# A vision tower in split fp32: weight low parts moved from VectorE to GpSimd, the opening cut in halves

## The reference

```python
h = L0_tok(x)                                    # patches @ W_lin + b, class token, positions
h = h + L0_attn(layernorm(h))                    # 16 heads of 64, causal
h = h + L0_ffn(layernorm(h))                     # 256 -> 1024 -> 256
h = h + L1_attn(layernorm(h))                    # 16 heads of 64, not causal
h = h + L1_ffn(layernorm(h))                     # 8 experts 256 -> 1024 -> 256, times masked logits
...
    h = jnp.einsum('bsd,df->bsf', x, w1) + b1    # L0_ffn
    h = float2fix(h, 8)                          # round to 1/256
    h = pwlin_gelu_basic(h, 8, 8)                # 33 knots of gelu, linear between, rounded
    out = jnp.einsum('bsf,fd->bsd', h, w2) + b2
    return float2fix(out, 8)
```

## Time and profile before

| | |
|---|---|
| median of 3 runs | 944.38 us (944.03 to 945.27) |
| the profiled execution | 946.15 us |
| its span, first to last instruction | 944.4 us |
| PE busy | 919.1 us, 97% |
| DVE busy | 586.4 us, 62% |
| ACT busy | 557.6 us, 59% |
| POOL busy | 155.6 us, 16% |
| mean DMA rate | 36 GB/s |

### The profile page before, as it was taken

The page is one execution under the profiler, slowest core; times in us unless marked ns, Lnnn a source line. Parts: engine busy times, 40 slices in busy tenths (PEclk is TensorE's granted clock), DMA queues, the critical chain, the costliest instruction groups (busy, mean ns, idle before and its releaser), DMA issues.

```text
span 944.4 us, 19121 instructions
## 1 busy us (share of the span) xinstructions
PE 919.1 (97%) x7073; PEld 856.1 (91%) x7073; DVE 586.4 (62%) x1860; ACT 557.6 (59%) x1571; POOL 155.6 (16%) x173
## 2 busy tenths in 40 slices
PE   8999999999999999999999999999999999999998
PEld 8978988788877878888879999999999999999998
DVE  4677676749999776757667787554354534554333
ACT  4666474647664755656555655565556646575442
POOL 0332122211000221222210000711011111111012
PEclk9999999999999999999999999999999999999999
DMA  9310000001100210000001012102020111100001
GB/s 334 135 46 1 2 1 2 2 1 46 45 1 3 87 45 1 2 1 2 2 28 64 1 45 90 46 2 90 1 91 1 46 45 46 46 1 1 2 14 39
DMA packets 8800, 34.43 MB, mean 36 GB/s; under 512 B 642, under 2 KB 5122, under 8 KB 5380
## 3 DMA queue, kind: packets, MB, share of 16 engines
q1 hardware_dynamic: 8708, 33.22, 9.8%
HBM read 32.00 MB, written 1.21 MB: 35 GB/s over the span
## 4 chain that ended last, share of the span: by engine, by line
PE 44%; issue 34%; DVE 13%; POOL 6%; ACT 2%; POOLq 0%; DVEq 0%; ACTq 0%
PE D L609 15%; PE O L609 10%; POOL h L372 4%; PE O L804 4%; PE S L779 3%; PE T L790 3%; PE S L609 3%; PE D L631 2%; DVE probsT L1364 2%; DVE probs L1349 2%; PE O L725 2%; PE O L878 1%; POOL h L384 1%; DVE xc L1240 1%; DVE rt L1231 1%
## 5 line engine op out<-in xcount | busy, mean ns | idle before, releaser
L1620 DVE TENSOR_TENSOR hid<-work,hid 128x296 fp32r<-128x296 f32 x256 | 134.3, 551 | 178.5 <-ACT hid L1157 177.7
L609 PE MATMUL O<-hid,wslot 128*128 128x296 f32 (+2 forms) x1680 | 238.4, 300 | 0.0
L609 PEld LDWEIGHTS O<-hid,wslot 128*128 128x128 f32 x1680 | 231.2, 188 | 0.6
L609 PE MATMUL D<-xn,wslot 128*128 128x296 f32 (+2 forms) x1368 | 219.9, 307 | 0.0
L609 PEld LDWEIGHTS D<-xn,wslot 128*128 128x128 f32 x1368 | 197.7, 190 | 3.2 <-issue 0.3
L1153 ACT ACTIVATE work<-D,prm 128x296 f32<-128x296 f32 x128 | 66.1, 516 | 166.2 <-PE D L609 165.8
L1048 ACT ACTIVATE probs<-probs,negmax 111x111 f32<-111x111 f32 (+1 forms) x352 | 130.3, 372 | 29.9 <-DVE negmax L1349 29.4
L588 POOL TENSOR_TENSOR probs<-probs,rsum 111x444 f32<-111x444 f32 (+1 forms) x88 | 81.3, 925 | 360.9 <-DVE rsum L1357 360.9
L609 PE MATMUL S<-xn,wslot 128*128 128x296 f32 (+2 forms) x864 | 133.6, 301 | 0.0
L609 PEld LDWEIGHTS S<-xn,wslot 128*128 128x128 f32 x864 | 123.0, 189 | 0.1
L1349 DVE CUSTOM_DVE_ANT_0 probs<-S,maska 111x111 f32<-111x111 f32 (+1 forms) x352 | 73.1, 263 | 66.3 <-PE S L779 66.3
(11 more groups left out here) (180 smaller groups left out, 1174.5 us busy)
## 6 DMA issues: line engine op xcount, KB each, us to landing
raw<-in_moe SPq DMA_DIRECT2D x16, 1024.0 KB, 4.8
raw<-in_attn SPq DMA_DIRECT2D x7, 1024.0 KB, 4.9
work<-in_x SPq DMA_DIRECT2D x2, 1008.0 KB, 8.2
out<-h SPq DMA_DIRECT2D x4, 296.0 KB, 2.6
w2f<-in_attn SPq DMA_DIRECT2D x1, 1024.0 KB, 13.5
raw<-in_ffn SPq DMA_DIRECT2D x1, 1024.0 KB, 5.0
w2f<-in_ffn SPq DMA_DIRECT2D x1, 1024.0 KB, 5.0
raw<-in_x SPq DMA_DIRECT2D x2, 504.0 KB, 5.1
```

Of the source, the lines that this page charges most:

```text
L609: mm = pe.matmul(psum, a, b, start=(first and k == 0), stop=(k == 3 * n - 1))
L1620: nc.vector.tensor_tensor(moe_hid(s, 1), moe_g(s)[:, 0:w], moe_hid(s, 0).bitcast(F32), ALU.subtract).then_inc(m_hid, 1)
```

## The change

**On POOL**, between the scaling of the first attention and that of the second, three whole pieces are subtracted: `FIRST_W` + 6, + 7 and + 8, each as soon as ACT's high part of it is there. DVE's twelve quarters for them go. PE and SP wait for the same pieces as before, on POOL's semaphore.

**In the opening** the second chunk's patches are loaded, copied and subtracted in halves (`x1_half`, new semaphores `x1_in`, `x1_high`, `x1_low`), PE embeds the second chunk half by half for both banks, 18 warm-up matmuls stand in the place of 28, `variance(0, 0)` stands one embedding later, and on DVE and ACT the last chunk's and the query weight's parts stand ahead of the first layer norm's end.

**The bias row** is prepared in two pieces: four copies at unit 3, the subtraction at unit 4.

```diff
...
         x0_in = sem("x0_in")
+        x1_in = sem("x1_in")
+        x1_high = sem("x1_high")
+        x1_low = sem("x1_low")
         v0_in = sem("v0_in")
...
         LATE_W = FIRST_W + 4
+        POOL_LATE = [FIRST_W + 6, FIRST_W + 7, FIRST_W + 8]
         NPIECE = FIRST_W + len(weights)
...
 
+            if i in POOL_LATE:
+                return (pool_split, LATE_W - NSTART + POOL_LATE.index(i) + 1)
             if i >= LATE_W:
-                return (dve_split, i - LATE_W + 1 - past(i))
+                return (dve_split, i - LATE_W + 1 - past(i) - sum(k < i for k in POOL_LATE))
             return (start_split, i + 1) if i < NSTART else (pool_split, i - NSTART + 1)
...
 
+        def x1_half(t, k):
+
+            n = KF * CHUNKS[1][1] // 2
+            return t[:, k * n:(k + 1) * n]
+
         def piece_size(i):
...
                     dst, src = w_half(dst, 1), w_half(src, 1)
-                if i == 1:
+                if i == 2:
+                    n = KF // 2
+                    sp.dma_start(x1_half(dst, 0).rearrange("p (k n) -> p k n", k=n),
+                                 src[:, 0:n, :]).then_inc(x1_in, 16)
+                    dst, src = x1_half(dst, 1).rearrange("p (k n) -> p k n", k=n), src[:, n:KF, :]
+                elif i == 1:
                     n = KF // 2
...
             normalise(0)
-
+            for i in POOL_LATE:
+                if place_free(i):
+                    pool.wait_ge(*place_free(i))
+                split(i)
             normalise(1)
...
             pe.wait_ge(consts, 1)
-            for _ in range(28):
+            for _ in range(18):
                 pe.matmul(BO[0][:, 0:P], mean_w[:, :], mean_w[:, :], start=True, stop=True)
...
                 embed_part(0, dc, range(KF // 2, KF), False, True)
-            embed(1, 0)
+            pe.wait_ge(x1_low, 1)
+            for dc in range(KD):
+                pe.wait_ge(h_set, dc + 1)
+                embed_part(1, dc, range(KF // 2), True, False)
             mean(0, 0)
-            embed(1, 1)
+            pe.wait_ge(*piece_split(2))
+            for dc in range(KD):
+                embed_part(1, dc, range(KF // 2, KF), False, True)
+            embed(2, 0)
             variance(0, 0)
-            for c in (2, 3):
-                for dc in range(KD):
-                    embed(c, dc)
+            embed(2, 1)
+            for dc in range(KD):
+                embed(3, dc)
             attention(0, 0)
...
             nc.scalar.activation(x0_half(piece_place(1)[0], 1), x0_half(piece_raw(1), 1), ACT.Copy).then_inc(high_ready, 1)
-            high_part(2)
+            act.wait_ge(x1_in, 16)
+            nc.scalar.activation(x1_half(piece_place(2)[0], 0), x1_half(piece_raw(2), 0), ACT.Copy).then_inc(x1_high, 1)
+            landed(act, 2)
+            nc.scalar.activation(x1_half(piece_place(2)[0], 1), x1_half(piece_raw(2), 1), ACT.Copy).then_inc(high_ready, 1)
             nc.scalar.preload_act_table_set("natural_log_exp_and_others")
...
 
-            square(0, 0)
             high_part(4)
-            inv_root(0, 0)
+            square(0, 0)
             high_part(FIRST_W)
+            inv_root(0, 0)
             high_part(FIRST_W + 1)
...
 
+            def low_x1(k):
+                dve.wait_ge(*((high_ready, 3) if k else (x1_high, 1)))
+                high, low = piece_place(2)
+                nc.vector.tensor_tensor(x1_half(low, k), x1_half(piece_raw(2), k), x1_half(high.bitcast(F32), k),
+                                        ALU.subtract).then_inc(start_split if k else x1_low, 1)
+
             def low_w(k):
...
             set_h(0, 0)
-            low_part(2)
+            low_x1(0)
             set_h(0, 1)
+            low_x1(1)
             low_part(3)
...
             low_part(4)
-            root = newton(0, 0)
             set_h(2, 0)
-            apply(0, 0, root)
-            set_h(2, 1)
             low_part(FIRST_W)
+            root = newton(0, 0)
+            set_h(2, 1)
+            apply(0, 0, root)
             set_h(3, 0)
...
 
-            def prepare():
+            def prepare_high():
 
...
                     nc.vector.tensor_copy(b1r[row:row + 1, :], b1row[row:row + 1, :]).then_inc(b1_ready, 1)
+
+            def prepare_low():
+
                 dve.wait_ge(b1_ready, 2)
...
                     clear_gaps()
-                else:
-                    for k in range(SPLITS):
-                        low_quarter(FIRST_W + 8, k)
                 add_halves(*ln_due(l, 0))
...
                         add_halves(*ln_due(l, u + 1))
-                    if u == 4:
-                        (prepare, prepare_gates)[l]()
+                    if l == 0 and u == 3:
+                        prepare_high()
+                    if l == 0 and u == 4:
+                        prepare_low()
+                    if l == 1 and u == 4:
+                        prepare_gates()
                     if l == 1 and u in (1, 2):
...
                         low_quarter(FIRST_W + W_FF, 2)
-                    if l == 0 and u == NUNIT:
-                        low_quarter(FIRST_W + 6, 0)
-                        low_quarter(FIRST_W + 6, 1)
                     if l == 1 and NUNIT - 2 <= u <= NUNIT:
...
                     ff_sum(p - 1)
-                if p == 1:
-                    low_quarter(FIRST_W + 6, 2)
-                    low_quarter(FIRST_W + 6, 3)
                 if p in (1, 2):
...
                 ff_out1(NC - 1, dc)
-            for k in range(SPLITS):
-                low_quarter(FIRST_W + 7, k)
             attention(1)
```

More of the change, by code:

```diff
@@ L1086, in attention @@
                         high_part(tail_weight(l)[u - (NUNIT - 3)])
+            high_part(4)
             square(0, 0)
-            high_part(4)
+            high_part(FIRST_W)
             inv_root(0, 0)
-            high_part(FIRST_W)
             high_part(FIRST_W + 1)
@@ L1283, in _ @@
             low_part(4)
+            set_h(2, 0)
+            low_part(FIRST_W)
             root = newton(0, 0)
-            set_h(2, 0)
+            set_h(2, 1)
             apply(0, 0, root)
-            set_h(2, 1)
-            low_part(FIRST_W)
             set_h(3, 0)
```

## The result

| | before | after |
|---|---|---|
| median of the runs, us | 944.83 (944.03 to 947.79, 4 runs) | 952.52 (952.4 to 953.55, 4 runs) |
| ratio, 95% interval | | 1.008 (1.0066 to 1.0093) |
| the profiled execution, its span | 946.15, 944.4 | 952.4, 950.6 |
| attention 1 begins, us | 34.16 | 31.85 |
| attention 2 begins, us | 301.65 | 309.62 |

The change costs 7.7 us. The median of before is 944.83 here and 944.38 above because a fourth run joined the three. The kernel is slower, as forecast, but the time lies above the range of 943.5 to 951.5. "Attention 1 begins" and "attention 2 begins" are the starts of PE's first projection of each in the profiled execution. By the begin of attention 2 all of the loss is there: 309.62 - 301.65 = 8.0.

What follows compares the result with a forecast made beforehand. PE was taken as the bound, busy nearly throughout, with DVE close behind in the feed-forward. The terms -2.0 - 0.2 - 1.3 + 4.2 + 2.8 + 0.7 = +4.2 us on 944.4 gave 948.6, range 943.5 to 951.5.

Steps and rivals of the forecast that it cites:

- opening: Shorter warm-up and halved second chunk: first attention begins at about 32.1, -2.0 us, bounds 1.2 and 2.8.
- bias row: First attention, units 3 and 4: copies go to unit 3, subtraction stays at unit 4; between 0 and -0.6, taken -0.2 us.
- query on POOL: Feed-forward, piece + 6: root step held +1.2 for DVE, but removed quarters shorten PE's waits of 0.70 and 0.98: -1.3 us.
- key on POOL: Feed-forward, piece + 7: L1495 held until about 271.5 where DVE has almost no idle time: +4.2 us for PE.
- value on POOL: Feed-forward, piece + 8: DVE held another 4.2 us, gaps give back some 1.4, last rounding comes later: +2.8 us.
- clock: PE's new waits of 2 to 3 us bring half clock behind them: between 0 and 3.4, taken +0.7 us.
- The hold: A two-SBUF-input DVE step waits for the end of POOL's SBUF-reading instruction: 0.43 to 4.3 us each, upper end taken.
- the port is let go: Rival, chance 0.20: port freed within POOL's long instruction, each piece costs about 0.43, -3.5 in all: 940.9 us.
- PE becomes slow for longer: Rival, chance 0.05: lower clock after each new wait, or the opening's first matmuls late: about 951 us.

Runs made afterwards that it cites:

- e3: e1 with only the query weight's low part on POOL, key and value in quarters on DVE: 941.70 us, ratio 0.9965 to before.
- e1: The changed kernel with opening and bias row only, all three low parts back in quarters on DVE: 942.29 us, ratio 0.9972 to before.
- e11: e1 with only the value weight's low part on POOL, query and key in quarters on DVE: 945.58 us, ratio 1.0008 to before.
- e14: The changed kernel, with POOL starting the value's piece only when the rounding PE waits for is done: 949.42 us, ratio 1.0043 to before.
- e6: e1 with the query and key weights' low parts on POOL, the value's in quarters on DVE: 946.94 us, ratio 1.0011 to before.
- e15: The changed kernel with matmuls without a reader in the first two of PE's three new feed-forward waits: 947.44 us, ratio 1.0028 to before.
- e2: The kernel before with the three low parts on POOL, without the opening and bias edits: 954.95 us, ratio 1.0099 to before.
- e5: The changed kernel, each of POOL's three low parts in four instructions instead of one: 948.68 us, ratio 1.0033 to before.
- e7: e1 plus one POOL subtraction that nobody needs, at the moment of the key's low part: 947.09 us, ratio 1.0009 to before.
- e8: e1 plus two POOL memsets, in place of the idle subtraction of e7: 943.93 us, ratio 0.9979 to before.
- e4: The changed kernel with matmuls without a reader in all three of PE's new feed-forward waits: 947.82 us, ratio 1.0035 to before.
- e12: e3 plus 12 matmuls without a reader in PE's wait in unit 3 of the second attention: 941.68 us, ratio 0.9960 to before.
- e13: e3 plus 6 matmuls without a reader in PE's wait in unit 3 of the second attention: 941.08 us, ratio 0.9956 to before.

## Why the prediction was wrong in size, and right in direction

By the begin of attention 2, in us, forecast and measured:

| step | forecast | measured | from |
|---|---|---|---|
| opening | -2.0 | -2.3 | attention 1 at 31.85 |
| bias row | -0.2 | -0.2 | the rest of 2.5; PE's wait of 0.59 at unit 4 is gone, one of 0.43 stands at unit 3 |
| query on POOL | -1.3 | -1.1 | e3 against e1 |
| key on POOL | +4.2 | +3.9 | down-projection at 274.90 against 274.72, where the one of 263.00 had stood 3.76 ahead of before |
| value on POOL | +2.8 | +2.8, +2.7 | e11 against e1, e14 against e6 |
| clock | +0.7 | +5.0 | after against e15 |
| sum | +4.2 | +8.0 | 309.62 - 301.65 (the rounded rows make 8.1) |

- **The hold** (the step "a DVE instruction with two SBUF inputs waits for the end of a POOL instruction that reads SBUF") was right: 1.98 and 4.31 us for the two-input steps. The 4.83 us of the third fell on a step that this sentence leaves out. Of the bounds 0.43 and 4.3 for each piece the upper end held (4.31 - 0.35 and 4.83 - 0.50); the query's 1.98 is shorter because that step began 3 us into POOL's instruction. The rival that the port is let go (940.9) is out; it was to decide by a step under 1.5 us.
- **The opening and the bias row** were right within 0.3. For the bias row there is no run by itself. The forecast that PE's wait for the second chunk shrinks to 0.4 came out at 0.53.
- **The query's piece** was right: the root step ended 1.5 later, and the first part of the feed-forward kept one wait of 0.61 out of 0.70 and 0.98.
- **The key's piece** was right in size and place of the wait, wrong in the step held: I named L1495 (L1531 with the change); it got in first and the root step behind it was held.
- **The value's piece** was right by itself (e11, e14). In the changed kernel the hold fell on the rounding, a one-input step that I had not counted among those that can be held ("about a step of the other kind between them"). That it fell there was the half clock's doing: e15, without it, has the hold one group of steps later.
- **The clock** is the step that failed. "Half a clock over a few microseconds of PE work costs up to 1.7 each; part of it would lie under DVE's chain. Between 0 and 3.4; I take +0.7." It cost 5.0, beyond even its upper bound, and it was priced as two short losses side by side, not as something that moves the next hold. Three things were missed. The first low stretch was 6.83 us, not 3.41 as in the trace of before, and it lay over the down-projection, which took 2.9 more; e6, where only this stretch is there, puts 2.0 of it on attention 2 (303.95 - 297.99 = 6.0, of which the hold is 3.9). Slow PE then delivered late what DVE needed, which moved the third hold onto the step that PE waits for and made a wait of 4.62. And that wait brought its own low stretch. The last two together are the remaining 3.0 (309.62 - 306.62, e14). These 3.0 needed both errors, the clock and the step kind: e15 takes away the first and e14 the second, by keeping POOL off the rounding, and either is enough to lose them.
- **The rival "PE becomes slow for longer"** at about 951 and 0.05 named what happened, with too low a chance and too low a price. Without the clock my sum is +3.5, and e15 measures +3.0. That the other terms agree so well is in part luck, as the key's held step was not the one I named.

What stays open: why the first low stretch is 6.83 us long in the change and in e2, e5, e6 and e14, but 3.41 in e7, where the first of the two waits is 1.09 in place of 1.63 to 2.03 us, and why the one behind the wait of 4.62 is 3.41 in the change and 6.83 in e2. No run varies that alone. Open is also which of DVE and POOL goes first when they start within 0.03 us of each other.

## What to carry to other kernels

Before giving POOL a long instruction that touches SBUF, take the whole instruction as time in which DVE's steps with two SBUF inputs, and its one-input casts and roundings in SBUF, stand still; look which DVE step will be next when POOL becomes free to start, and who waits for that step. Where POOL's start can be set by a semaphore, set it behind the step that PE needs, not in front of it. A wait of 2 us on PE is not priced by its length alone: count the work behind it at half rate and follow what that delays. Where nothing better is at hand, a few matmuls without a reader in the wait are cheap, if they are shorter than it.

## What the runs showed of the hardware

- A held step ends 0.2 to 0.4 us after the POOL instruction that held it (seven cases in after, e7, e11, e14 and e15, steps of 1.98 to 4.88 us).
- DVE can be held by a memset on POOL too, if its step is a cast: 1.27 in place of 0.35 (e8).
- The hold works in both directions: POOL's subtraction took 5.27 to 5.44 where two-input DVE steps ran on for 0.9 to 1.05 us beside its start (second piece of after, e11, e15), and 4.50 to 4.58 where the DVE step under way had at most 0.13 us left or an input in PSUM.
- POOL in four instructions of 128 x 512 did not free DVE: its steps took 1.05 to 1.62 us each, and one 2.40 (e5).
- PE's granted clock fell to 0.50 at two waits of 2.0 and 2.3 us close together (after, e2, e6, e14), of 1.6 and 2.3 (e5) and of 1.1 and 2.3 (e7), at one of 4.62 (after, e2), and in two profiled executions (before, e3) behind one of 1.6, which the other profiled executions that I read there (after, e1, e4, e6, e14, e15) had without a fall. With the waits filled it did not fall, in any profiled execution (e4, e12, e13, e15). Inside the span it lasted 3.41 or 6.83 us each time.
